# AdaLN block with two attentions on one core: the middle stage in halves of 256 tokens and six iterations

## The reference, cut to what matters

```
h = _layernorm(x) * (1 + ca) + sa
x = x + ga * favor(h, Wq, Wk, Wv, Wo, bo, proj)      # num / den per token and head, then Wo
h = _layernorm(x) * (1 + cb) + sb
for e in range(4):                                   # 512 tokens each
    xn = _layernorm(h[e]) * norm_w + norm_b          # the norm inside the second attention
    m = 256 >> e
    q, k, v = xn[..., :m] @ q_w[:, :m].T + q_b, ...
x = x + gb * (softmax(q k^T * d**-0.5) v @ o_w[:m, :m].T + o_b[:m] + h)
```

## Time and profile before

| | before |
|---|---|
| median of 3 runs (lowest, highest) | 2008.32 us (2004.5, 2009.01) |
| the profiled execution, its own time | 2007.16 us |
| its span | 2005.4 us |
| busy in the span: PE, DVE, ACT, POOL | 87%, 72%, 54%, 59% |
| mean granted TensorE clock | 0.934 of full |

### The profile page before, as it was taken

The page is one execution under the profiler, slowest core; times in us unless marked ns, Lnnn a source line. Parts: engine busy times, 40 slices in busy tenths (PEclk is TensorE's granted clock), DMA queues, the critical chain, the costliest instruction groups (busy, mean ns, idle before and its releaser), DMA issues.

```text
span 2005.4 us, 31471 instructions
## 1 busy us (share of the span) xinstructions
PE 1750.5 (87%) x11520; PEld 997.9 (50%) x11520; DVE 1450.5 (72%) x2617; ACT 1083.1 (54%) x1998; POOL 1179.5 (59%) x974
## 2 busy tenths in 40 slices
PE   5698869999899886999979977799997988599997
PEld 3576434444377543444447744344435764344443
DVE  4686777777478577777648857777766876787774
ACT  0586333656578432566648823266665863336564
POOL 0685354666768346566768723666676853546666
PEclk8898978999999897999989989899998989889999
DMA  4000043001110025101020003500111000430011
GB/s 126 1 2 1 18 158 85 17 11 39 53 33 2 1 72 167 30 9 48 1 85 2 2 1 117 140 12 17 41 34 52 2 2 0 171 89 16 12 37 43
DMA packets 55714, 87.56 MB, mean 44 GB/s; under 512 B 13188, under 2 KB 32004, under 8 KB 52868
## 3 DMA queue, kind: packets, MB, share of 16 engines
q1 hardware_dynamic: 55560, 85.54, 14.5%
HBM read 49.68 MB, written 35.70 MB: 43 GB/s over the span
## 4 chain that ended last, share of the span: by engine, by line
PE 65%; DVE 14%; ACT 10%; issue 4%; POOL 3%; DMA 2%; SPq 2%; POOLq 0%; ACTq 0%; DVEq 0%
PE PS L1175 12%; PE PS L1300 11%; PE PS L1288 9%; PE PS L1313 5%; PE PS L1069 5%; DVE MXP L861 4%; PE PS L1096 3%; PE PS L1077 3%; PE PS L1218 3%; PE PS L1106 3%; ACT HT L525 2%; ACT HTR L528 2%; PE PS L1245 2%; DVE QKS L911 2%; ACT PHIQ L563 2%
## 5 line engine op out<-in xcount | busy, mean ns | idle before, releaser
L498 POOL TENSOR_TENSOR TS<-PR 128x1024 f32<-128x1024 f32 (+1 forms) x256 | 573.1, 2239 | 336.7 <-ACT PR L664 336.7
L861 DVE TENSOR_REDUCE MXP<-PS 128x1 f32<-128x512 f32 x960 | 598.0, 680 | 202.7 <-PE PS L1175 199.3
L664 ACT ACTIVATE PR<-PS 128x512 f32<-128x512 f32 x960 | 504.8, 602 | 425.9 <-PE PS L1288 422.4
L1175 PE MATMUL PS<-KOP,QOP 96*128 96x512 f32 x960 | 422.8, 460 | 45.1 <-DMA KOP<-k_scr 34.2
L1288 PE MATMUL PS<-QOP,KOP 97*128 97x512 f32 x960 | 379.4, 409 | 18.1 <-ACT PR L664 12.7
L1175 PEld LDWEIGHTS PS<-KOP,QOP 96*128 96x128 f32 x960 | 190.7, 200 | 300.3 <-DVE MXP L861 174.7
L1300 PE MATMUL PS<-PR,V 128*32 128x512 f32 x1920 | 273.1, 606 | 0.0
L1288 PEld LDWEIGHTS PS<-QOP,KOP 97*128 97x128 f32 x960 | 181.3, 192 | 85.6 <-ACT PR L664 50.2
L445 POOL TENSOR_TENSOR RSTD<-VE,minus_half 128x4 f32<-128x4 f32 x32 | 33.9, 1060 | 237.6 <-DVE VE L758 237.6
L1313 PE MATMUL PS<-TS,ones 128*32 128x512 f32 x960 | 133.2, 593 | 5.4 <-POOL TS L498 5.4
L1069 PE MATMUL PS<-W1T,HTR 128*128 128x512 f32 x384 | 115.1, 438 | 21.2 <-POOL HTR L402 21.0
(11 more groups left out here) (144 smaller groups left out, 2691.0 us busy)
## 6 DMA issues: line engine op xcount, KB each, us to landing
KOP<-k_scr SPq DMA_DIRECT2D x84, 256.0 KB, 6.0
k_scr<-QKS SPq DMA_DIRECT2D x64, 256.0 KB, 2.8
QOP<-q_scr SPq DMA_DIRECT2D x180, 64.0 KB, 2.0
q_scr<-QKS SPq DMA_DIRECT2D x40, 256.0 KB, 2.8
X<-in_L_attn_x_dram SPq DMA_DIRECT2D x16, 512.0 KB, 4.8
out_dram<-X SPq DMA_DIRECT2D x16, 512.0 KB, 3.1
QOP<-MXT SPq DMA_DIRECT2D x240, 0.5 KB
KOP<-k_scr SPq DMA_DIRECT2D x48, 64.0 KB, 2.0
```

Of the source, the lines that this page charges most:

```text
L498: g.tensor_tensor(sums(k)[:, 0:len(stage)], pair[:, :, 0], pair[:, :, 1], ALU.add).then_inc(S["psum_t"], 1)
L664: a.activation(PR[:, k % 2, w, q], bank(score_bank(p, n, w, q)), ACT.Exp).then_inc(S["ex"], 1)
L861: v.tensor_reduce(MXP[:, u % 2, i, kc:kc + 1], bank(max_bank(p)), AX.X, ALU.max).then_inc(S["am_rd"], 1)
L1175: mm(bank(max_bank(p)), QOP[0:96, u % QS6, i * P:(i + 1) * P], KOP[0:96, h % KS6, kc * CH:(kc + 1) * CH], start=True, stop=True).then_inc( ...
```

## The change

- Order of the slots: experts 3, 1, 0, 2 instead of 3, 0, 1, 2.
- The middle stage works in halves `h` of 256 tokens: `centred(s, h)`, `merged(s, h)` and so on. PE has six iterations instead of seven: the projection of slot `it - 2` follows its transposes in the same iteration. DVE and ACT keep seven; the last has only leftovers.
- The second norm is two instructions of DVE for each 128 tokens, (x - mean) * scale and then * deviation + shift, 128x256 each; POOL's L471 and DVE's L924 are gone. The third norm goes from DVE to ACT (`centred`), with the negated mean times the deviation as bias, which POOL computes.
- The value bias is no longer added to V but folded into the output bias at the start (`OBE`, by five more matmuls), and ACT copies V. The low part is read straight from PSUM, so `TMP` goes.
- PSUM: banks 0 to 4 for slot `it`, and a ring of three (5 to 7) for transposes, blocks and values.
- Keys of head 0 go straight from `QKS` to `KOP` for slots 1 to 3.
- Unit 0's row maxima reach `QOP` by four PE products with `ident`, one ACT copy, and no DMA.
- `SUM` has memory of its own. Half of the output base is left for POOL during the slots 1 to 18 of the third stage (`PIECES`), each piece 256 tokens.
- The last features of the first stage go through banks 3 and 4 instead of bank 6 alone.

```diff
-    expert = (3, 0, 1, 2)
+    expert = (3, 1, 0, 2)
...
+    PIECES = (1, 2, 3, 4, 5, 6, 7, 10, 12, 14, 16, 18)
...
+        def kinds(s):
+
+            qk = [("q", s, n) for n, _ in blocks(s)]
+            return [("x", s, h) for h in range(2)] + qk[:2] + [("v", s, 0)] + qk[2:] + [("v", s, 1)]
...
+        def ring(kind):
+
+            return 5 + place[kind] % 3
...
+                        if s > 0 and t == 0:
+                            sp.wait_ge(S["num"], 2 * NC * (b + 1))
+                            for r, half in ((0, 0), (32, 0), (64, 1)):
+                                sp.dma_start(KOP[r:r + DH, 0, e * CH:(e + 1) * CH].bitcast(F32),
+                                             QKS[0:DH, n % 3, half].bitcast(F32)).then_inc(S[f"kf{e}"], 16)
...
+                def deviations_again(s, h):
+                    cols, n = halves(s, h), 2 * (NC * b + s) + h + 1
+                    wait_all(pool, (S["ve3"], 2 * n))
+                    g.tensor_tensor(RSTD[:, cols], VE[:, cols], minus_half[:, cols], ALU.pow).then_inc(S["rs3"], 1)
+                    wait_all(pool, (S["rs3"], n))
+                    g.tensor_tensor(NMR[:, cols], NEGM[:, cols], RSTD[:, cols], ALU.mult).then_inc(S["nmr3"], 1)
...
+                    if k in PIECES:
+                        e, step, t0 = pieces[PIECES.index(k)]
+                        output_base(e, step, t0, t0 + 2)
...
+                def centred(s, h):
+                    m = D if expert[s] == 0 else P
+                    act.wait_ge(S["nmr3"], 2 * (NC * b + s) + h + 1)
+                    if s > 0:
+                        act.wait_ge(S["x2T"], 2 * (NC * b + s - 1) + h + 1)
+                    for i in (2 * h, 2 * h + 1):
+                        t = s * TPC + i
+                        a.activation(X2[:, i, 0:m], Hh[:, t, 0:m], ACT.Identity, bias=NMR[:, t:t + 1],
+                                     scale=RSTD[:, t:t + 1]).then_inc(S["x2"], 1)
...
+                def high_qk(s, some):
+                    for n, t in some:
+                        act.wait_ge(S["qp"], NQ * b + n + 1)
...
+                        a.activation(QKS[:, n % 3, 0], bank(ring(("q", s, n))), ACT.Identity, bias=qk_bias(t)
+                                     ).then_inc(S["q_hi"], 1)
...
+                            if u == 0:
+                                v.tensor_reduce(MXN[:, 0, 0:TPC], MXP[:, 0], AX.X, ALU.max, negate=True
+                                                ).then_inc(S["top"], 1)
+                                continue
...
+                def modulated(s, h):
+                    dve.wait_ge(S["rstd2"], 2 * (NC * b + s) + h + 1)
+                    counted = [mark(v.scalar_tensor_tensor(Hh[:, t], X[:, t], MV[:, t, 0:1], MODB[:, b, 2, :],
+                                                           ALU.subtract, ALU.mult)) for t in halves(s, h)]
+                    for t, count in zip(halves(s, h), counted):
+                        dve.wait_ge(S["dve_own"], count)
+                        v.scalar_tensor_tensor(Hh[:, t], Hh[:, t], RSTD[:, t:t + 1], MODB[:, b, 1, :], ALU.mult,
+                                               ALU.add).then_inc(S["h2"], 1)
...
+                def low_parts(s, some):
+                    for n, t in some:
+                        dve.wait_ge(S["q_hi"], NQ * b + n + 1)
+                        v.scalar_tensor_tensor(QKS[:, n % 3, 1], bank(ring(("q", s, n))), qk_bias(t),
+                                               QKS[:, n % 3, 0].bitcast(F32), ALU.add, ALU.subtract
+                                               ).then_inc(S["q_lo"], 1)
...
+                    first, second, third = it < NC, 0 <= it - 1 < NC, 0 <= it - 2 < NC
                     if it >= 4:
                         maxima((it - 4) * EARLY, (it - 3) * EARLY)
...
+                    if first:
+                        reciprocals(it)
+                    if second:
+                        modulated(it - 1, 1)
+                    if third:
+                        low_parts(it - 2, blocks(it - 2)[:2])
+                    if first:
+                        merged(it, 0)
+                    if second:
+                        statistics_of_h(it - 1, 0)
...
-                dve.wait_ge(S["base"], NC * (b + 1))
...
+                        if p >= 3:
+                            pe.wait_ge(S["am_rd"], NU * MAXU * b + p - 2)
...
+                    if third:
+                        second_qk(it - 2, blocks(it - 2)[:2])
+                        second_values(it - 2, 0)
...
+                        projected(it, 0)
+                        projected(it, 1)
                     if it >= 3:
...
+                        maxima((it - 3) * EARLY, (it - 2) * EARLY)
+                    if third:
+                        second_values(it - 2, 1)
...
+                pe.wait_ge(S["top"], b + 1)
+                pe.wait_ge(S["q_lo"], NQ * (b + 1))
+                pe.wait_ge(S["v2_sb"], 2 * NC * (b + 1))
+                for i in range(TPC):
+                    last = mm(PS[96:97, 7, i * P:(i + 1) * P], MXN[:, 0, i:i + 1], ident[:], start=True, stop=True,
+                              tile_position=(0, 96))
+                last.then_inc(S["top_ps"], 1)
```

More of the change, by code:

```diff
@@ L83, in adaln_block @@
     SHN = [len(range(i, NU, QS6)) for i in range(QS6)]
+    SHD = [len(range(i or QS6, NU, QS6)) for i in range(QS6)]
     LOOK, EARLY = 24, 4
@@ new lines, in normal @@
+                def normal(s, h):
+                    e, cols = expert[s], slice(2 * P * h, 2 * P * (h + 1))
+                    if s > 0:
+                        act.wait_ge(S["vp"], 2 * (NC * b + s))
+                        act.wait_ge(S["qp"], NQ * b + blocks(s)[0][0])
+                    act.wait_ge(S["x2T"], 2 * (NC * b + s) + h + 1)
+                    for k in range(depth(s)):
+                        weight, bias = ((COLM[:, e - 2, 0:1], COLM[:, e - 2, 1:2]) if e >= 2 else
+                                        (COLS[:, 0, k:k + 1], COLS[:, 1, k:k + 1]))
+                        a.activation(XNT[:, k, cols], bank(ring(("x", s, h)))[:, 2 * P * k:2 * P * (k + 1)], ACT.Identity, bias=bias,
+                                     scale=weight).then_inc(S["xn_sb"], 1)
@@ L1041, in _ @@
             last.then_inc(S["mod"], 1)
+            pe.wait_ge(S["wT_sb"], 8)
+            pe.wait_ge(S["vb_ok"], KD)
+            for e in range(EXPERTS):
+                o, m = sum(width[:e]), width[e]
+                ks, rows = range(KD if e == 0 else 1), min(width[e], P)
+                for k in ks:
+                    last = mm(bank(3)[:, o:o + m], VBC[0:rows, k], OWT[0:rows, k, 0:m], start=k == 0,
+                              stop=k == len(ks) - 1)
+            last.then_inc(S["obm"], 1)
             for b in range(B):
-                pe.wait_ge(S["wT_sb"], 8)
                 if b >= 2:
@@ new lines, in second_qk @@
+                def second_qk(s, some):
+                    pe.wait_ge(S["xn_sb"], xns(b, s) + 2 * depth(s))
+                    for n, t in some:
+                        j, w = t % 2, (1 if t < 2 else 0)
+                        pe.wait_ge(*freed(b, ("q", s, n)))
+                        for k in range(depth(s)):
+                            last = mm(bank(ring(("q", s, n))), W2T[:, k, w * D + j * P:w * D + (j + 1) * P], XNT[:, k],
+                                      start=k == 0, stop=k == depth(s) - 1)
+                        last.then_inc(S["qp"], 1)
```

546 lines of the change are left out of this document (287 added, 259 removed).

## The result

The changed kernel takes 1913.68 us (median of 4 executions, 1908.03 to 1914.23) against 2007.55 us (the three executions shown above and a fourth of 2006.78): a ratio of 0.9523 [0.9511, 0.9535]. The direction and most of the mechanism held. The size did not.

The account below looks back on a forecast made before the run. No engine is full, so waits between engines set the middle stage's length. 2005.4 - 73.2 (18.3 a batch) + 3 + 2 = 1937.2, and 1.8 outside the span: 1940 us against medians; own range 1928 to 1955, whole range 1918 to 1974.

Parts of the forecast that it names:

- End of the first stage, -3.2: Before the denominators: freed banks remove waits for ACT's copies, so the denominators start 3.2 us earlier a batch.
- Iteration 0 is the same chain over all engines, 13.2 us: First iteration of the middle stage: keeps its earlier length of 13.2 us.
- the low clock doesn't come: Rival, chance 0.15: dense PE makes expert 0's blocks 6.9 instead of 9.9 us, iteration 0 2 us shorter; 1920 us.
- Iterations 1 to 3, "bound by DVE", 12.3 + 14.3 + 14.3: Middle stage: DVE's added-up stream without holes sets the pace, 12.3 us then 14.3 us twice, ending at 250.4.
- The rival of double cost: Rival, chance 0.12: DVE's 32 new scale-and-shift instructions a batch take 0.65 instead of 0.38 us; 1974 us.
- The wait at p = 3: Iteration 3's end: PE's fourth maxima product waits from about 245 to 251.1 until DVE has read the first.
- Iterations 4 and 5, 27.4 to p8: Middle stage from PE's entry at 252.5 to DVE's p8 at 279.9, expert 0's eight blocks at low clock, 9.9 us.
- The last maxima and the score product: End of the middle: DVE sets the pace at 0.62 us a maximum; score product at 290.0 against 308.34.
- Setup, +3: Kernel start: five more products, 1.8 us, and six small DVE instructions, 1.4 us, cost 3 us.
- Pieces in the softmax slots, +2: Third stage: POOL's twelve moved pieces are nearly hidden, 0.5 us a batch, 2 in all; 58 without cover.
- The DMA wait: Rival, chance 0.10: the slot order makes slots 2 and 3 each wait 5 us more for DMAs; 1980 us.
- The bounds of DVE's iteration, -15 and +20: Middle stage: a full DVE iteration of 14.3 us may be 13.0 to 16.0, moving the total by -15 to +20.

Follow-up runs that it names:

- run 1: Changed kernel with the last two groups of features through bank 6 again, all three groups ahead of the transposes of the sums: 1933.21 us, 0.9626.
- run 2: Changed kernel with the last features through bank 6 again, plus fourteen unused identity products laid into PE's waits there: 1924.47 us, 0.9584.
- run 3: Kernel before, with only banks 3 and 4 for the last features, bank 2 for the sums' transposes, these ahead of the last group: 1982.73 us, 0.9873.
- run 9: Changed kernel with PE's products of values done twice in both halves of iterations 2 and 3: 1931.78 us, 0.9609.
- run 10: Changed kernel with DVE's subtract-and-scale of each half done twice in iterations 2 and 3: 1918.8 us, 0.9548.
- run 4: Changed kernel with 3, 7 and 11 early maxima in iterations 3 to 5 instead of 4, 8 and 12, on PE and DVE: 1893.09 us, 0.9428.
- run 5: Changed kernel with head 0's keys of slots 1, 2 and 3 going through DRAM again: 1933.62 us, 0.9626.
- run 6: Changed kernel with unit 0's row maxima going by DVE's transpose and four DMAs again: 1925.6 us, 0.9582.

## Why the prediction was off

The miss is 26 us in the direction of more gain, 25.7 by the spans. By the table: 19.7 in the middle (4.9 a batch), 5.0 between the last score and the next denominators, 2.3 in the third stage, less 1.3 in the rest, most of it ahead of batch 0's denominators. In batch 0 the 4.9 are -2.8 in iteration 0, +0.4 from there to the second reciprocals, -2.1 in DVE's stream, +0.9 at PE's entry into iteration 4, -1.6 in iterations 4 and 5, and +0.3 in the last maxima. Point by point:

**End of the first stage, -3.2: mis-sized.** From the products with `PK` to the denominators it gave -4.0 in batch 0 (186.91 to 196.09 before, 191.93 to 197.09 now) and -3.5, -4.4 and -4.4 in the others; the -4.9 of the table hold some 0.8 more, which lie ahead of this stretch. The order of events was right, and the waits that go are those of the earlier trace rows. But I left the transposes of `DENS` 1.09 long, as at the low clock of before, and the copies behind them likewise; measured are 0.85 and 0.60 for four, and 0.56 of waiting where 1.00 was. By runs 1 and 2 most of it is the waits and their order, and one at least is the clock.

**"Iteration 0 is the same chain over all engines, 13.2 us": this step failed.** It takes 10.4. The step took the duration from before together with the clock that before had there (0.50), although the change removes the holes of PE just ahead of it. I had seen it as a rival ("the low clock doesn't come") with 0.15, but tied it to the blocks of expert 0 and bound its two halves together. In fact one half came true by itself: iteration 0 ran at full clock, while expert 0's blocks saw a mixed one. Four kernels make a table of it, iterations 0 and 1 together, average of four batches:

| | low clock at the start | full clock |
|---|---|---|
| order of before | 24.5 (before) | 21.7 (run 3) |
| order of the change | 23.0 (run 1) | 21.0 (the change) |

So the clock is worth 2.0 to 2.8 of the 3.5 us, and the new order, in halves of `RB` and `MT`, 0.7 to 1.5. Over the whole middle the clock is worth less: run 1 has 0.5, within what single executions scatter by, since what the clock gives at the start is in part taken back at the end.

**Iterations 1 to 3, "bound by DVE", 12.3 + 14.3 + 14.3: wrong bound, and 2.1 too long.** DVE's stream took 11.3, 13.6 and 14.0, as the times between its reciprocals (211.25, 222.52, 236.10) and its first maxima (250.06) show. The single costs were nearly right: 0.43 for each scale-and-shift (0.87 for two) where I took 0.38, and 0.75 for a low part where I took 0.69. The row L741 had the 0.43 in it: 0.16 and 256 columns at 1.04 ns. The rival of double cost is dead. Nor does the rule that the prediction cites with it (the Trainium skill, Vector Engine (DVE) Microarchitecture Reference, section 7) show as a loss against row L741; of what rate it means the half, no run here tells. What I added on top, 1.0 for waits on its own results, was too much: with the single costs as measured (+0.3 and +0.2) the sum of 13.3 gives 13.8, and nothing is left for it. And the pace of iterations 2 and 3 is PE's, which I named as "the other bound of this step" and did not follow: up to p = 3 run 9 loses 2.5 of the 2.6 added to PE, run 10 only 2.2 of the 3.7 added to DVE (1.3 by the medians of the whole kernel). Iteration 1 was not tested.

**The wait at p = 3: right.** "PE waits until 251.1" on the predicted clock; with 4.2 for the later start of the middle and -4.5 from the two steps above, 250.8, which is the row's start. That the row lies so near 251.1 is luck: a start that came 4.2 too late met two steps that were 4.5 too long. The order of events is not luck. The wait is 4.86 where I had some 6. Run 4 shows that it costs what it shows: 5.6 a batch without it. It was in the forecast as a fact of the change, and taking it away is the cheapest gain left.

**Iterations 4 and 5, 27.4 to p8: 25.8.** The blocks of expert 0 took 5.37 + 3.60 = 8.97 in place of 9.9, between the forecast and the rival's 6.9. The clock over 252 to 260 is 0.71 where the earlier trace rows had 0.57. Why it is low there stays open: run 4 has no hole at p = 3, and its blocks are as slow. PE's entry came 0.9 later after the wait than I had it (1.91 of values stand between).

**The last maxima and the score product: right in size.** 10.4 from p8 to the score against 10.1, at 0.62 a maximum. "From here DVE sets the pace" holds up to the tiny products; behind them PE at the low clock sets it in batch 0. Run 1, at full clock there, takes 8.5 from its last wait to the score where the changed kernel takes 9.6. Both parts behind it were worth what the argument needed: without the direct keys +5.2 a batch (I had expected 3.5 in that run), without the tiny products +2.5 (2.4).

**Setup, +3: +5.0 in the profiled execution, and not a fixed number.** Windows of the changed kernel over the first tiles:

```profile
70.00:80.00 10.00, 7.41 (x35) 5.15 (x35) 3.31 (x4) 3.94 (x9) 2.43 (x5) 0.69 0.00 0
```

and of run 5, with the same setup:

```profile
70.00:80.00 10.00, 7.28 (x51) 5.30 (x50) 4.97 (x7) 6.12 (x13) 3.38 (x6) 0.98 0.00 0
```

With the high clock it does 51 products where the other does 35, and its denominators come 2.3 us earlier, at 194.8: that is +2.7 of setup. The rest of the +5.0 goes with the low clock in the first tiles.

**Pieces in the softmax slots, +2: no cost shows** (first to last score 224.4 against 224.5 on average, where single batches differ by 2), so the cover named for them holds. **The DMA wait** as a rival did not occur: in the middle of batch 0 ACT waits for no DMA, and the loads of the direct keys land in 2.0 us in the changed kernel too, as the earlier trace rows let me expect.

**The range.** The bounds of DVE's iteration, -15 and +20, would give the forecast case 1925 to 1960 and not 1928 to 1955. The whole range ended at 1918 because the high clock was one rival worth 20 us, and nothing was set aside for several of the terms being too long at once.

Taken together, for a change of 94 us: the banks some 25 (run 3), the direct keys 20 (run 5), unit 0's maxima without a DMA 12 (run 6). The other 37 or so go to what was not undone by itself: the slot order, the halves and the iteration less, the fused scale and shift, the third norm on ACT and the pieces out of the middle. How they share it is open. The sum also presumes that the parts add, which run 1 (19.5 for the same banks) shows only roughly.

## What to carry to other kernels

A duration read from a stretch at the low clock must not be carried over as a constant when the change fills PE's holes ahead of that stretch: price it at both levels, stretch by stretch, give each its own chance, and expect a part of it to come back elsewhere. When products go ahead of their readers in a ring of n banks, queue at most n in one group; the product n + 1 stops everything behind it on an in-order engine until the reader's next turn, and one number (4 to 3) was worth 26 us here. When two engines are both over 90% busy, don't choose the bound by adding up one of them: add a known amount of work to each, and see which is lost in full and where. An engine with slack can still be the one that is waited for at the end.
